# The transpose of xn in the first work bank, and a new order of work on every engine, in an attention and slot-mixture kernel

## What is computed

```python
# attention: 16 heads of 8
q, k = exp(xh @ Wq.T + bq), exp(xh @ Wk.T + bk);  v = xh @ Wv.T + bv      # xh = layernorm(x)
kv  = cumsum(k[:, :, :, None] * v[:, :, None, :], axis=1)                # per head 8x8, summed over the tokens so far
out = einsum('zsD,zsDd->zsd', q, kv) / sum(q * cumsum(k, axis=1))
x   = x + layernorm(out @ Wo.T + bo)
# mixture over 512 slots
xn  = rms_norm(layernorm(x));  logits = xn @ slots.T
disp = softmax(logits over the 8 experts);  s = disp.T @ xn
proc = gelu(s @ w1) @ w2
x   = x + layernorm(softmax(logits over all 512 slots) @ proc)
```

## Time and profile before

| | |
|---|---|
| median of three runs | 642.82 us |
| the profiled execution | 642.81 us, its span 641.1 us |
| TensorE matmul busy | 584.1 us (91%) |
| weight loads busy | 523.2 us (82%) |
| VectorE busy | 475.6 us (74%) |
| ScalarE busy | 468.9 us (73%) |
| GpSimd busy | 453.3 us (71%) |

### The profile page before, as it was taken

One profiled execution on the slowest core, in us unless ns is written; L12 is line 12 of the kernel. 1 busy time (PEld: TensorE's weight loads), 2 busy tenths in 40 slices (PEclk: granted clock), 3 DMA queues, 4 the chain that ended last, 5 costly groups with the idle time before them and its releaser, 6 DMA issues.

```text
span 641.1 us, 11538 instructions
## 1 busy us (share of the span) xinstructions
PE 584.1 (91%) x4136; PEld 523.2 (82%) x4136; DVE 475.6 (74%) x929; ACT 468.9 (73%) x1097; POOL 453.3 (71%) x469
## 2 busy tenths in 40 slices
PE   2347899999999999999999999999999999999996
PEld 1236788898888888988888888988888889888885
DVE  6676878777778778777788787777787787777631
ACT  3335787777778877778777877777788777777765
POOL 4987677777887778777877777778877787765100
PEclk9999999999999999999999999999999999999999
DMA  3000000000000000000000000000000000000000
GB/s 107 8 17 10 16 13 22 27 26 26 26 18 17 26 18 25 27 26 26 26 10 26 20 24 26 26 25 26 20 15 27 17 26 26 18 17 9 9 10 16
DMA packets 16828, 14.34 MB, mean 22 GB/s; under 512 B 2850, under 2 KB 16644, under 8 KB 16772
## 3 DMA queue, kind: packets, MB, share of 16 engines
q1 hardware_dynamic: 14708, 12.76, 6.7%
q10 hardware_dynamic: 2064, 0.86, 0.5%
HBM read 5.25 MB, written 4.19 MB: 15 GB/s over the span
## 4 chain that ended last, share of the span: by engine, by line
PE 66%; DVE 22%; POOL 4%; ACT 4%; issue 4%; DMA 0%; SPq 0%; DVEq 0%; POOLq 0%; ACTq 0%
PE HB L676 17%; DVE WB L887 12%; PE LA L658 10%; PE LA L689 8%; PE LA L637 4%; PE WB L609 4%; PE WB L534 3%; PE HB L666 3%; PE WB L610 3%; PE LB L647 2%; DVE att L897 2%; PE WB L593 2%; DVE xnT_lo L860 2%; PE WB L560 2%; ACT xnT_hi L387 2%
## 5 line engine op out<-in xcount | busy, mean ns | idle before, releaser
L676 PE MATMUL HB<-w_c,hid 128*128 128x128 f32 x1024 | 129.8, 275 | 1.4 <-ACT hid L391 1.4
L676 PEld LDWEIGHTS HB<-w_c,hid 128*128 128x128 f32 x1024 | 125.7, 191 | 4.9 <-ACT hid L391 2.2
L872 DVE TENSOR_TENSOR prod<-WB,E 128x1024 f32<-128x1024 f32 (+1 forms) x96 | 90.8, 946 | 9.5 <-PE WB L610 8.7
L306 POOL TENSOR_TENSOR kv<-E 128x1024 f32<-128x1024 f32 x32 | 68.4, 2138 | 41.0 <-ACT E L387 40.8
L313 POOL TENSOR_TENSOR kv_lo<-kv,kv_hi 128x1152 fp32r<-128x1152 f32 x32 | 84.8, 2652 | 9.3 <-ACT kv_hi L387 9.3
L887 DVE TENSOR_REDUCE WB<-prod 128x288 f32<-128x2304 f32 x32 | 82.0, 2562 | 3.2
L355 POOL TENSOR_TENSOR kv<-kv,kv_prev 128x1024 f32<-128x1024 f32 x32 | 76.6, 2395 | 0.0
L391 ACT ACTIVATE hid<-HB 128x512 f32<-128x512 f32 x128 | 70.7, 600 | 3.7 <-PE HB L536 3.4
L306 POOL TENSOR_TENSOR kv_prev<-prev 128x1024 f32<-128x1024 f32 x32 | 68.3, 2134 | 0.4 <-DMA prev<-E 0.4
L318 POOL TENSOR_TENSOR own<-E,own 128x128 f32<-128x128 f32 x32 | 17.5, 545 | 70.0 <-DVE own L880 70.0
L387 ACT ACTIVATE disp<-LA 128x512 f32<-128x512 f32 x64 | 34.7, 594 | 43.6 <-PE LA L637 43.6
(11 more groups left out here) (134 smaller groups left out, 1520.2 us busy)
## 6 DMA issues: line engine op xcount, KB each, us to landing
X<-in_L_attn_x_dram SPq DMA_DIRECT2D x32, 128.0 KB, 2.1
out_dram<-res SPq DMA_DIRECT2D x32, 128.0 KB, 2.0
prev<-E SPq DMA_DIRECT2D x32, 112.0 KB, 2.1
w_in<-in_L_ffn_w_dram ACTq DMA_DIRECT2D x2, 256.0 KB, 4.5
prev<-E SPq DMA_DIRECT2D x32, 15.0 KB, 2.0
se_in<-n_L_ffn_slot_embeds_dram ACTq DMA_DIRECT2D x1, 256.0 KB, 3.5
w_in<-in_L_attn_Wq_dram SPq DMA_DIRECT2D x1, 64.0 KB, 2.4
w_in<-in_L_attn_Wk_dram SPq DMA_DIRECT2D x1, 64.0 KB, 2.2
```

The source lines that it names most:

```text
L306: return pool.tensor_tensor(dst.rearrange("p (d h e) -> p d h e", d=HD, h=NH), k.rearrange("p (o h e) -> p o h e", o=1, h=NH).broadcast_to ...
L676: last = pe.matmul(PR[:, j, :], hid[:, f, j * P:(j + 1) * P], w2_c[:, f, :], start=(f == 0), stop=(f == FJ - 1))
L872: dve.tensor_tensor(prod[u][:, :, d0 * DIM:d1 * DIM].rearrange("p c (d f) -> p c d f", d=g), WB[:, k % 2, 0:g * DIM].rearrange("p (o d f) ...
```

## The change

The transpose of xn goes to the first bank of `WB`, behind the third causal unit of the following batch (it waits for `prod_ready[UN - 1]` and no longer for `prod_ready[1]`); both parts are read from there. The reduction of `attention` loses its wait for `xnT_lo_ready`. `x_transpose` gains a wait for it, and others gain waits that an earlier order made needless. The lists of all five engines are put in another order:

```diff
@@ SyncE
-                if z is not None:
-                    store(z, z % 2)
+                if a is not None:
+                    store(a, a % 2)
@@ GpSimd: the list of a step
-  x1_rstd_of(l), own_value(r), pair_sum(t), o_rstd_of(a), own_product(t), sums_low(t), outer_even(p),
-  x_rstd_of(q), slot_norms(t), y_rstd_of(r), outer_odd(p), wo_order(t)
+  slot_norms(r), own_value(r), pair_sum(t), o_rstd_of(a), wo_order(r), sums_low(t), x_rstd_of(q),
+  outer_even(p), y_rstd_of(r), outer_odd(p), own_product(t), x1_rstd_of(r)
@@ ScalarE
             def sums_high(n):
-                after(act, cum_done[UN - 1], n - 1)
             def xnT_high(n):
-                copy(xnT_hi[:, :], WB[:, 1, 0:SEQ]).then_inc(xnT_hi_ready, 1)
+                copy(xnT_hi[:, :], WB[:, 0, 0:SEQ]).then_inc(xnT_hi_ready, 1)
-  xT_high(p), gelu(b) 0, gelu(b) 1, sums_high(t), gelu(b) 2, gelu(b) 3
+  gelu(b) 0, gelu(b) 1, xT_high(p), gelu(b) 2, sums_high(t), gelu(b) 3
@@ TensorE
             def x_transpose(n):
+                after(pe, v_copied, n - 1)
+                after(pe, xnT_lo_ready, n - 3)
             def attention_out(n):
-                if n >= NB - 2:
-                    after(pe, attT_ready, n)
-                if n == 0:
-                    after(pe, v_copied, 2)
-                    after(pe, attT_ready, 0)
+                after(pe, v_copied, n + 2)
+                after(pe, attT_ready, n)
             def cumulate(n, k):
+                after(pe, v_copied, n + 1)          # k = 0 and k = 1
             def xn_transpose(n):
                 after(pe, xn_ready, n)
-                after(pe, prod_ready[1], n + 1)
-                    last = pe.transpose(WB[:, 1, c * P:(c + 1) * P], xn[n % 2][:, c, 0:DIM], ident[:, :])
+                after(pe, prod_ready[UN - 1], n + 1)
+                    last = pe.transpose(WB[:, 0, c * P:(c + 1) * P], xn[n % 2][:, c, 0:DIM], ident[:, :])
             # subtract_max, mixture: their waits hold for every batch, not for the last ones alone
-  ... x_transpose(p), logits(l), hidden(b) 2 3, att_transpose(r), wo_transpose(r), slot_transpose(r), project(p),
-  process(b) 2, 3, part_transpose(l), attention_out(r), cumulate(t) 0, process(b) 0, dispatch_transpose(l) ...
+  ... x_transpose(p), slot_transpose(r), hidden(b) 2 3, logits(l), att_transpose(r), project(p), process(b) 3, 2,
+  wo_transpose(r), part_transpose(l), attention_out(r), process(b) 0, cumulate(t) 0, dispatch_transpose(l) ...
@@ VectorE
             def attention(n, u):
                 after(dve, prod_ready[UN - 1], n)
-                after(dve, xnT_lo_ready, n - 1)
             def xnT_low(n):
-                low_part(xnT_lo[:, :], WB[:, 1, 0:SEQ], xnT_hi[:, :]).then_inc(xnT_lo_ready, 1)
+                low_part(xnT_lo[:, :], WB[:, 0, 0:SEQ], xnT_hi[:, :]).then_inc(xnT_lo_ready, 1)
-  slots_scale(b), multiply(r) 1, x1_normalise(l), slT_low(b), own_sum(r), multiply(r) 2, xnT_low(l), attention(r),
-  xT_low(p), bo_centre(p), slot_squares(p), slot_scale(r), part_maxima(l), w1_parts(t), slot_maxima(l),
-  token_maxima(l), wo_centre(r), second_residual(a), x_statistics(q), slot_parts(r), w2_centre(p),
-  multiply(t) 0, x_normalise(q), first_residual(r)
+  slots_scale(b), multiply(r) 1, multiply(r) 2, x1_normalise(l), slT_low(b), own_sum(r), xnT_low(l), attention(r),
+  slot_scale(r), slot_squares(t), xT_low(p), x_statistics(q), part_maxima(l), slot_maxima(l), w1_parts(p),
+  token_maxima(l), slot_parts(r), w2_centre(r), second_residual(a), wo_centre(r), x_normalise(q), bo_centre(p),
+  first_residual(r), multiply(t) 0
```

More of the change, by code:

```diff
@@ L357, in step @@
             def step(z, a, b, l, r, t, p, q, w):
-                if l is not None:
-                    x1_rstd_of(l)
                 if r is not None:
+                    slot_norms(r)
                     own_value(r, r % 2)
@@ L365, in step @@
                     o_rstd_of(a)
+                if r is not None:
+                    wo_order(r)
                 if t is not None:
-                    own_product(t, t % 2)
                     sums_low(t)
+                if q is not None and q > 0:
+                    x_rstd_of(q)
                 if p is not None:
                     outer_even(p, p % 2)
[L371 to L374, removed]
                 if r is not None:
@@ L379, in step @@
                 if t is not None:
-                    wo_order(t)
+                    own_product(t, t % 2)
+                if r is not None:
+                    x1_rstd_of(r)
             pipeline(pool, step)
@@ L478, in step @@
                     o_squares(a)
+                if b is not None:
+                    gelu(b, 0)
+                    gelu(b, 1)
                 if p is not None:
@@ L481, in step @@
                 if b is not None:
-                    gelu(b, 0)
-                    gelu(b, 1)
+                    gelu(b, 2)
                 if t is not None:
@@ L640, in subtract_max @@
             def subtract_max(n):
-                if n >= NB - 2:
-                    after(pe, tok_ready, n)
+                after(pe, tok_ready, n)
                 for g in range(2):
@@ L680, in mixture @@
             def mixture(n, u):
-                if n == NB - 1:
-                    after(pe, proc_ready, n)
-                    after(pe, comb_ready, n)
-                    after(pe, res_ready, n - 1)
+                after(pe, proc_ready, n)
+                after(pe, comb_ready, n)
+                after(pe, res_ready, n - 1)
                 for c in range(NC):
@@ L701, in step @@
                     x_transpose(p)
+                if r is not None:
+                    slot_transpose(r)
+                if b is not None:
+                    hidden(b, (2, 3))
                 if l is not None:
                     logits(l)
-                if b is not None:
-                    hidden(b, (2, 3))
                 if r is not None:
                     att_transpose(r)
-                    wo_transpose(r)
-                    slot_transpose(r)
                 if p is not None:
@@ L712, in step @@
                 if b is not None:
+                    process(b, 3)
                     process(b, 2)
-                    process(b, 3)
+                if r is not None:
+                    wo_transpose(r)
                 if l is not None:
@@ L718, in step @@
                     attention_out(r)
+                if b is not None:
+                    process(b, 0)
                 if t is not None:
                     cumulate(t, 0)
-                if b is not None:
-                    process(b, 0)
                 if l is not None:
@@ L957, in step @@
                     multiply(r, r % 2, 1)
+                    multiply(r, r % 2, 2)
                 if l is not None:
@@ L963, in step @@
                     own_sum(r, r % 2)
-                    multiply(r, r % 2, 2)
                 if l is not None:
@@ L968, in step @@
                     attention(r, r % 2)
+                    slot_scale(r)
+                if t is not None:
+                    slot_squares(t)
                 if p is not None:
                     xT_low(p)
-                    bo_centre(p)
-                    slot_squares(p)
-                if r is not None:
-                    slot_scale(r)
+                if q is not None and q > 0:
+                    x_statistics(q)
                 if l is not None:
                     part_maxima(l)
-                if t is not None:
-                    w1_parts(t)
+                    slot_maxima(l)
+                if p is not None:
+                    w1_parts(p)
                 if l is not None:
-                    slot_maxima(l)
                     token_maxima(l)
                 if r is not None:
-                    wo_centre(r)
+                    slot_parts(r)
+                    w2_centre(r)
                 if a is not None:
                     second_residual(a, a % 2)
+                if r is not None:
+                    wo_centre(r)
                 if q is not None and q > 0:
-                    x_statistics(q)
+                    x_normalise(q)
+                if p is not None:
+                    bo_centre(p)
                 if r is not None:
-                    slot_parts(r)
-                if p is not None:
-                    w2_centre(p)
+                    first_residual(r)
                 if t is not None:
                     multiply(t, t % 2, 0)
-                if q is not None and q > 0:
-                    x_normalise(q)
-                if r is not None:
-                    first_residual(r)
             pipeline(dve, step)
```

5 lines of the change are left out of this document (2 added, 3 removed).

## The result

| | before | after |
|---|---|---|
| median | 642.5 us (20 runs, 640.7 to 644.5) | 639.89 us (20 runs, 634.48 to 644.76) |
| ratio | | 0.9952, 95% interval 0.9934 to 0.9970 |
| the profiled execution | 642.81 us | 638.97 us, its span 637.1 us |
| usual step | 18.17 us | 17.78 us |
| long steps | none | nine, of 18.13 to 19.11 us |

The change makes the kernel 0.5% faster: 2.6 us by the medians, where 10 were forecast, and inside the range. The usual step is the one that the prediction worked out (17.79), but by two errors that cancel: the gain is 0.48 a step and not 0.38, and 0.09 of it is lost again on the way through SyncE. What was not foreseen are nine steps in two stretches (84 to 215 us and 464 to 501 us) that are up to 1.3 us longer, 8.0 us in all: they sum to 168.0, and nine usual steps to 160.0. Steps are counted from one transpose of xn to the next.

The account below looks back on a forecast made before the run. TensorE was taken to bound 28 steps of 18.17 us; gains of 0.18 and 0.20 make 17.79, 10.6 us in all, giving 632.2, plus 0.3 for the store's path: 632.5 us, range 628.5 to 643.

Parts of the forecast that it names:

- the store ahead of the shifts: SyncE's queue: shifts go out behind the early store, landing 2.1 us later; x1_normalise left with no slack and no loss.
- The bound and its two gaps: TensorE bounds each step; it idles 0.56 us ahead of the attention's transpose and 0.20 us ahead of cumulate 0.
- The wait removed, 0.18: VectorE's reduction in attention: dropping its wait for xnT_low gains 0.18 us a step, bounded by 0 and 0.20.
- multiply 2 ahead of x1_normalise: VectorE: delays slT_low, so hidden starts 0.30 us later; TensorE's way and VectorE's then end together, allowing only 0.18 gain.
- logits behind hidden 2 and 3: covered: TensorE: same matmuls, no time gained or lost; logits end near 309.5 and VectorE looks for them at 310.3.
- x_statistics ahead of the maxima: VectorE: delays the token maxima by 0.50 us; the dispatch exponentials stay hidden from TensorE by 0.6 us.
- process 0 ahead of cumulate 0, 0.20: TensorE: 0.89 us of matmuls cover the wait for the token maxima; gain 0.20 us a step, bounded by 0 and 0.26.
- x_normalise beside outer_even: VectorE is held by GpSimd's outer_even on the shared port until 315.3; costs nothing, with 0.4 us of cover.
- Rival 1: The path through SyncE binds mildly, 0.1 to 0.35 us over a step: 635.5 to 641.5 us; chance 0.15.
- Rival 2: Slow store issues and landings on SyncE's path make the kernel slower, 671 us; with only five stores, 639.5; chance 0.14.
- Start and end: 0: First steps and the last step with logits: no net gain or loss together, with 1.5 us either way.

Follow-up runs that it names:

- e1: The changed kernel with the store of batch z again, a step later than in the change, nothing else different: 629.4 us, ratio 0.9801.
- e10: e1 with the wait of attention for the low part of xn's transpose put back: 634.5 us, ratio 0.9875.
- e7: Kernel before with xn's transpose in the first bank, the reduction's wait removed, and multiplication 2 ahead of x1_normalise: 640.3 us, ratio 0.9970.
- e11: e7 with logits also moved behind hidden 2 and 3, ScalarE's list still old: 668.2 us, ratio 1.0404.
- e14: e11 plus process 0 ahead of cumulate 0 and ScalarE's list of the change; VectorE's end of step, GpSimd's and SyncE's lists old: 628.6 us, ratio 0.9781.
- e6: Kernel before with one edit, process 0 ahead of cumulate 0: 634.5 us, ratio 0.9869.
- e5: e1 with cumulate 0 ahead of process 0 again, as before the change: 634.5 us, ratio 0.9877.
- e3: The changed kernel with the early store kept, but the shifts ahead of it in SyncE's list: 629.7 us, ratio 0.9801.
- e2: Kernel before with one line of the change, the store of batch a and not z: 643.1 us, ratio 1.0007.
- e4: The changed kernel with the store of batch z, but the shifts held until the result that the early store waited for: 636.7 us, ratio 0.9927.
- e9: The changed kernel with 80 further satisfied waits at the start of TensorE's program, nothing in a step changed: 637.3 us, ratio 0.9912.

## Why the prediction was right, and where it failed

The time fell by a quarter of what was forecast, 2.6 us and not 10.3. The step that failed is the store ahead of the shifts, called without loss; it cost 10.5 us (e1). Two further errors, in the place of the logits and in the size of process 0's gain, do not show in the usual step.

**The bound and its two gaps.** Right. Both stalls of the earlier trace rows were where the time was. In the complete change nothing but these and the path through SyncE moved the step.

**The wait removed, 0.18.** Right: 0.19 (e10).

**multiply 2 ahead of x1_normalise.** Right in its mechanism: hidden starts 0.28 later (e7) and not 0.30, and both ways end together, 4.99 us behind the transpose of xn. Incomplete in that it stopped at TensorE: the late hidden also makes a late gelu, and ScalarE's copy of the attention stands behind it (0.11, e7).

**logits behind hidden 2 and 3: covered.** This step failed, though the sum hid it. I asked only who waits for the logits and not what the logits had covered. They stood where hidden 2 otherwise waits 0.96 us for gelu 0 (e11), and as long as they stand ahead of hidden 2 and 3 the attention's copy is late (e7). Their place is worth 0.15 a step together with ScalarE's list (18.12 to 17.97) and costs 0.97 without it (18.12 to 19.09). ScalarE's new order, which I costed nowhere, is what makes the difference between 668 and 636 us. In the complete change the two errors cancel.

**x_statistics ahead of the maxima.** Right: no idle time for it on TensorE, and e14, with the old order there, has the same step as e1.

**process 0 ahead of cumulate 0, 0.20.** Right in place, low in size: 0.29 in the kernel before (e6), which is past my upper bound of 0.26, and 0.22 in the changed one (e5). The term was mis-sized because I let cumulate 0 start 0.11 behind the last matmul of the projection, and it can start 0.03 behind. With 0.19 + 0.29 the step would be 17.69, and that is what e1, e3 and e14 have; I had 17.79. That after has 17.78 is luck: this error and the 0.09 lost through SyncE cancel.

**x_normalise beside outer_even.** Right: 1.86 us for two (0.60 for two of this shape otherwise), in nearly every step; outer_even ran from 313.53 to 315.67, and the two normalisations from 314.14 to 316.00. first_residual follows at 316.36, where I had 316.1. No cost: e14, in the old order, has the same step as e1. The rule of the Trainium skill that the prediction weighed (SBUF — State Buffer, Who interferes with whom) holds in every such step, and costs nothing where it falls.

**The store ahead of the shifts: no slack left, and no loss.** This is the step that made the forecast wrong. Its points in time are met within 0.12 us (store 314.25 for 314.14, shift 314.71 for 314.62, outer_odd 317.42 for 317.3), and yet x1's rstd ends 0.1 late, at 321.51, and hidden waits 0.16 for slT_lo: 0.09 of it stay in the step, 2.5 us, for which I had added 0.3 to the sum. The larger part is the term of 2.1 us for the landing. I took the median of the earlier trace rows and put it where the slack is zero; the same line has a maximum of 4.0. Landings of 2.5 to 3.4 us and issues of up to 2.2, in runs of neighbouring steps, cost 8.0 us. The tile's own spread did not announce this: in the kernel before, one landing of its 64 took over 2.2 us (the one of 4.0, at 259 us, with a packet beside it). What did was the load and the store, whose landings took 2.7 to 3.2 us in seven neighbouring steps from 118 to 227 us, with the packet beside them. Rival 1 has the mechanism and, with 635.5 to 641.5, the time. Rival 2's "only five of the stores, 639.5" is close by number, but not by cause: the store's issues are all 0.35 us, and it is the shifts that took long.

**Start and end: 0.** They gave 1.6 us (2.2 at the start, -0.6 at the end), just past the 1.5 that I had set. The 2.2 isn't known well: at the end of the second step before is at 86.4 us and e2, with the same full steps, at 85.5, so single executions differ there by about 1 us.

**The sum, redone.** The 27 full steps behind the second: 27 x 0.39 = 10.5, less 8.0 for the long ones, plus 1.6 for the ends: 4.1; the spans of the two profiled executions differ by 4.0. The place of the store turned a gain of 13 us, which e1 and e14 have, into 2.6: 8.0 by slow landings and long issues, 2.5 by the slack that was missing in every step.

## What to carry to other kernels

- Where a path is left with no slack, its latency is not its median. Cost it with the spread that the trace has, of the other transfers too, and ask whether the slow cases come singly or in a row.
- A block of work that is moved on one engine gives up what it covered there. Ask for the old gap before asking who waits for the block; the order of the engine that answers must be moved in the same edit.
- The pace inside a group of matmuls does not say how soon the next group can follow it: look for the same pair of groups elsewhere in the trace.
- In an in-order transfer queue, put the issue that waits for the latest result behind those whose landing is needed first.

## What the runs showed of the hardware

- **Instruction packets delay transfers.** 16 KB a packet, about one a step. With one beside them, prev's transfers landed in 2.5 to 3.5 us and not in 2.1, and the two issues took up to 2.81 us and not 1.44. In the kernel before, the packets met load and store instead, with landings of 3.1 and 3.2 us and a store's issue of 1.80, where nothing waited. 80 instructions more at the start of the program moved the places of the packets by 58 us, and the start of the second stretch of long steps from 464 to 406 us. The Trainium skill (Runtime: NRT & Kernel Launch, Instruction fetch mechanics) says that an engine's instructions are refilled in blocks of 16 KiB, 256 instructions, over a DMA queue, and that the cost of crossing a block is mostly hidden. The size agrees with the 0.54 MB in 33 packets here; and TensorE's 8272 matmuls and weight loads would make 32 such blocks, an estimate from that page by which these are the packets of TensorE's program. TensorE was busy for 17.65 of 17.68 us in a step of e14, so for the engine itself nearly nothing showed; for transfers beside the packet, it was not hidden.
- **A wait on the same engine's last instruction** costs 0.19 us: 0.53 from start to start and not 0.34 (e10).
- **A group of matmuls can be followed faster than its own pace.** Matmuls of 128x128 are 0.11 us apart in process 0, the transpose behind them started 0.11 behind the last of them (before), and cumulate 0 (128x512) 0.03 behind (e6).
- **TensorE's clock** was at the lower of its levels for part of the second step in e4 and e9 (granted clock 0.80 in 8.6 us) and at the full one in after; it cost 1.5 us there.
